# A decayed scan with layer norm and a quantized feed-forward layer: another first stage, with eight scan matmuls a batch instead of ten and a partial sum on GpSimd

## What is computed

```python
x = x + layernorm(x) * r
h = relu(quant_linear(layernorm(x), w1, b1))     # w1: 2048 x 512
x = x + quant_linear(h, w2, b2)                  # w2: 512 x 2048
# quant_linear: input rounded to 0..255 steps of s_in = max(input)/255 over the WHOLE input,
#   weight rounded to int8 with a scale per output channel, bias rounded to steps of s_in*s_w
```

## Time and profile before

| | |
|---|---|
| median of three runs | 1306.49 us |
| the profiled execution, its own time | 1307.37 us |
| its span, first to last instruction | 1305.6 us |
| mean granted TensorE clock, share of full speed | 0.979 |
| busy: PE, DVE, ACT, POOL | 1229.4, 909.8, 992.6, 291.0 us |
| moved by DMA | 460.23 MB, 353 GB/s in the mean |
| last operations on y in the first stage (DVE) end | 344.5 us |
| first hidden product starts | 358.7 us |
| second stage's last sums, third stage's first product | 832 us, 838.4 us |

### The profile page before, as it was taken

How to read it: one execution, slowest core, us unless ns; L and a number is a source line. 1 busy time by engine, 2 the same in 40 slices (tenths; PEclk the granted TensorE clock), 3 DMA queues, 4 the chain that set the end, 5 groups by cost and what they waited for, 6 DMA issues and landing times. The chain is left out here.

```text
span 1305.6 us, 17104 instructions
## 1 busy us (share of the span) xinstructions
PE 1229.4 (94%) x5386; PEld 564.2 (43%) x5386; DVE 909.8 (70%) x1314; ACT 992.6 (76%) x1403; POOL 291.0 (22%) x777
## 2 busy tenths in 40 slices
PE   6768999999599999999999999799999999999998
PEld 2333443434344444444444444344444444444443
DVE  5979999999667777777777777555545545444446
ACT  5688787877767777777777776688888777778794
POOL 2859999999600000000000000000000000000000
PEclk9888999999899999999999999899999999999999
DMA  9887999997489999999999997699999999999997
GB/s 356 330 320 262 343 335 349 328 350 287 184 298 358 368 350 347 363 362 361 349 354 363 363 356 297 246 341 414 415 415 415 415 415 416 415 416 416 416 352 260
DMA packets 136127, 460.23 MB, mean 353 GB/s; under 512 B 10852, under 2 KB 10872, under 8 KB 123512
## 3 DMA queue, kind: packets, MB, share of 16 engines
q1 hardware_dynamic: 82680, 276.86, 54.0%
q10 hardware_dynamic: 53376, 182.47, 39.3%
HBM read 266.35 MB, written 192.94 MB: 352 GB/s over the span
## 5 line engine op out<-in xcount | busy, mean ns | idle before, releaser
L881 PE MATMUL ps<-w2T,xq 128*128 128x512 f16 x2048 | 450.2, 381 | 11.9 <-ACT xq L593 11.4
L839 PE MATMUL ps<-xq,w1T 128*128 128x512 f16 x2048 | 449.8, 381 | 1.4 <-DVE xq L717 1.4
L593 ACT ACTIVATE xq<-xq,hb,hs 128x512 f16<-128x512 f32 x494 | 358.5, 802 | 83.2 <-PE ps L881 61.6
L708 DVE TENSOR_REDUCE work<-xq 128x2 f32<-128x1024 f32 x255 | 311.0, 1220 | 127.0 <-ACT xq L546 127.0
L546 ACT ACTIVATE xq<-ps 128x1024 f32<-128x1024 f32 x255 | 260.9, 1023 | 123.8 <-PE ps L839 123.5
L818 PE MATMUL ps<-xq,work 128*128 128x512 f32 x640 | 291.3, 613 | 30.0 <-ACT xq L481 19.6
L881 PEld LDWEIGHTS ps<-w2T,xq 128*128 128x128 f16 x2048 | 199.3, 98 | 262.8 <-ACT xq L593 26.0
L839 PEld LDWEIGHTS ps<-xq,w1T 128*128 128x128 f16 x2048 | 199.5, 98 | 237.7 <-issue 3.3
L818 PEld LDWEIGHTS ps<-xq,work 128*128 128x128 f32 x640 | 122.8, 195 | 196.1 <-issue 146.1
L756 DVE TENSOR_TENSOR work<-ps,cs_bc 128x512 f32<-128x512 f32 x128 | 87.1, 689 | 98.0 <-PE ps L881 90.8
L481 ACT ACTIVATE xq<-ps,rstd 128x512 f32<-128x512 f32 x128 | 77.9, 688 | 62.1 <-POOL rstd L448 56.3
(11 more groups left out here) (105 smaller groups left out, 577.4 us busy)
## 6 DMA issues: line engine op xcount, KB each, us to landing
hidden_scratch<-xq SPq DMA_DIRECT2D x240, 512.0 KB, 6.1
xq<-hidden_scratch ACTq DMA_DIRECT2D x220, 512.0 KB, 19.8
xq<-in_x_dram SPq DMA_DIRECT2D x32, 1024.0 KB, 7.8
x_scratch<-xq SPq DMA_DIRECT2D x32, 1024.0 KB, 5.7
xq<-in_ctx_dram ACTq DMA_DIRECT2D x31, 1024.0 KB, 5.6
work<-x_scratch ACTq DMA_DIRECT2D x29, 1024.0 KB, 7.9
work<-x_scratch SPq DMA_DIRECT2D x25, 1024.0 KB, 8.3
out_dram<-work SPq DMA_DIRECT2D x24, 1024.0 KB, 15.0
```

Of the source, the lines that this page charges most:

```text
L593: act.activation(hq[c % HQ], src[:, c % 2, :], ACT.Relu, bias=hb[:, q:q + 1], scale=hs[:, q:q + 1]).then_inc(h_scaled, 1)
L708: dve.tensor_reduce(hmax[:, b * NF + 2 * q:b * NF + 2 * q + 2], src, AX.X, ALU.max).then_inc(kept_maxed, 1)
L839: last = pe.matmul(bank, w1T[:, k, f * P:(f + 1) * P], xq_rows(b, k), start=(k == 0), stop=(k == KD - 1))
L881: last = pe.matmul(acc_bank(s, i), src[:, i * P:(i + 1) * P], w2T[:, q, :], start=first, stop=final)
```

## The change

The numbers of the first stage are made another way. ACT adds the negative mean to `x` in place and makes `1 + rstd * scan` from PSUM, and DVE makes `y = (x - mean) * (1 + rstd * scan)` in one multiplication with a row maximum. This y lacks the row's mean of `x`, which the second layer norm does not see; the means are kept in `nmean1` and subtracted when the bias is added to the output (`scalar_tensor_tensor` in place of `tensor_tensor`, 128 instructions). All `bn_stats` of `x` are DVE's, three batches ahead. GpSimd makes mean and deviation of two batches together, on 8 columns. It also makes `carried = 0.9^128 * kv0 + kv1` of each batch's squares, in two operations on 128x512, so that tiles 2 and 3 need two and three matmuls: 1+2+2+3 = 8. The scan rotates through six PSUM banks. Weights come in eight quarters of 1 MB, one every second batch from batch 2 on, and both weights are done inside the stage. `x` has eleven slots and `ctx` three; the last eleven batches of y stay in their slots, are quantized first and straight from there, and six of them are stored to DRAM in the second stage only. PE turns a quantized batch tile by tile as the tiles come.

```diff
-XS = 4
-ACT_TILES = 2
-AHEAD = 2
-
+XS = 11
+CS = 3
+RING = 4
+LATE = 6
+LEAD = 5
+BIAS_AT = 21
 HELD = 2
 NXQ = 3
 NKEEP = 12
 XC = 4
+NX = 3
...
+    parked = list(range(NB - XS, NB))
+    order_b = [b for n in range(XS - NX, XS) for b in parked if b % XS == n]
+    order_b += [b for b in parked if b not in order_b]
+    order_b += list(range(NB - XS))
+    late = list(range(NB - LATE, NB))
...
+    x_groups = [[0], [1]] + [[j, j + 1] for j in range(2, NB, 2)]
+    y_groups = [[j, j + 1] for j in range(0, NB - 2, 2)] + [[NB - 2], [NB - 1]]
+    x_group = {j: g for g, js in enumerate(x_groups) for j in js}
+    y_group = {j: g for g, js in enumerate(y_groups) for j in js}
+    quarters = [(w, k) for w in range(2) for k in range(4)]
+
+    def weights_at(j):
+        m = j // 2 - 1
+        return [m] if j % 2 == 0 and 0 <= m < len(quarters) else []
...
+            def load_x(j):
+                if j == XS - 1:
                     sp.wait_ge(dve_step, 1)
-                if not is_first(j, XS):
-                    sp.wait_ge(x2_stored[n], g * 16)
-                sp.dma_start(xt[n], x_rows[bass.ds(j, 1)].rearrange("b p i d -> (b p) i d")).then_inc(x_loaded[n], 16)
-                for w, h in weight_halves(j):
-                    rows = (NF, KD)[w]
-                    part = slice(h * rows // 2, (h + 1) * rows // 2)
-                    sp.dma_start(w_stage[w].rearrange("p (c d) -> p c d", c=rows)[:, part, :],
-                                 (w1_rows, w2_rows)[w][:, part, :]).then_inc(w_loaded[w][h], 16)
-                if isinstance(j, int) and j == 2:
+                if j >= XS:
+                    sp.wait_ge(stats2_in, j - XS + 1)
+                    x2_is_stored(sp, j - XS)
+                sp.dma_start(xt[j % XS], x_rows[j]).then_inc(x_loaded[j % XS], 16)
+
+            def load_weights(m):
+                w, k = quarters[m]
+                wait_count(sp, w_int, m - 1)
+                if w == 0:
+                    sp.dma_start(w_stage[m % 2].rearrange("p (c d) -> p c d", c=4), w1_rows[:, 4 * k:4 * k + 4, :]).then_inc(w_loaded[m % 2], 16)
+                else:
+                    sp.dma_start(w_stage[m % 2], w2_rows[:, k, :]).then_inc(w_loaded[m % 2], 16)
+
+            def store_x2(b):
+                sp.wait_ge(x2_done, (b + 1) * NI)
+                sp.dma_start(x2_dram[b], xt[b % XS].rearrange("p i d -> p (i d)")).then_inc(x2_stored[b % XS], 16)
...
+            for j in range(NB):
+                if j + LEAD < NB:
+                    load_x(j + LEAD)
+                for m in weights_at(j + 2):
+                    if m > 0:
+                        load_weights(m)
+                if j > 0 and j - 1 not in late:
...
+                if order_b[b] in late:
+                    store_x2(order_b[b])
...
-            def second_stats(j, n):
-
-                cols = bass.ds(j * NI, NI)
-                wait_count(gp, stats2_ready, j)
-                gp.wait_ge(stats2_in, j + 1)
-                mean = pw2[:, 8, :]
-                var = row_stats(pw2, st2[:, n], mean, ln2_step, j * 4)
-                gp.wait_ge(ln2_step, j * 4 + 4)
-                gp.tensor_tensor(pw2[:, 9, :], var, var, ALU.add)
-                gp.tensor_tensor(zrow[:, cols], rowmax[:, n, :], mean, ALU.subtract).then_inc(stats2_used, 1)
-                gp.tensor_tensor(mean2[:, cols], pw2[:, 0, :], half[:, :], ALU.mult)
...
+            def x_stats(g):
+                js = x_groups[g]
+                wait_count(gp, stats1_ready, g)
+                gp.wait_ge(stats1_in, js[-1] + 1)
+                var = row_stats(pw1, stats_of(st1, js), nmean1[:, columns(js)], neg_half)
+                gp.tensor_tensor(rstd1[:, columns(js)], var, neg_half[:, 0:len(js) * NI], ALU.pow).then_inc(stats1_ready, 1)
+
+            def y_stats(g):
+                js = y_groups[g]
+                wait_count(gp, stats2_ready, g)
+                gp.wait_ge(stats2_in, js[-1] + 1)
+                var = row_stats(pw2, stats_of(st2, js), mean2[:, columns(js)], half)
+                gp.tensor_tensor(zrow[:, columns(js)], stats_of(rowmax, js), mean2[:, columns(js)], ALU.subtract)
+                gp.tensor_tensor(rstd2[:, columns(js)], var, neg_half[:, 0:len(js) * NI], ALU.pow).then_inc(stats2_ready, 1)
+
+            def carry(j):
+                gp.wait_ge(ctx_squared, j + 1)
+                wait_count(gp, scan_ready, (j - 1) * NI)
+                into, kv = carried[j % 2], ct[j % CS]
+                step(gp.tensor_scalar(into[:, 0, :], kv[:, 0, :], DECAY ** P, None, ALU.mult))
+                gp.tensor_tensor(into[:, 0, :], into[:, 0, :], kv[:, 1, :], ALU.add).then_inc(carry_ready, 1)
...
+            carry(0)
+            x_stats(x_group[0])
+            x_stats(x_group[1])
+            for j in range(NB):
+                if j % 2 == 1 and j + 1 < NB:
+                    x_stats(x_group[j + 1])
+                if j + 1 < NB:
+                    carry(j + 1)
+                if j % 2 == 0 and j >= 2:
+                    y_stats(y_group[j - 1])
+                for m in weights_at(j):
+                    round_weights(m)
+            y_stats(y_group[NB - 2])
...
-            def tile_stats(j, n, g):
-
-                for m, i in enumerate(range(NI - ACT_TILES, NI)):
-                    at = j * (2 * ACT_TILES) + 2 * m
-                    if m == 0:
-                        act.wait_ge(x_loaded[n], (g + 1) * 16)
-                    wait_count(act, act_step, at)
-                    mean = st1[:, n, i, 1:2]
-                    act.activation(unused, xt[n][:, i, :], ACT.Copy, scale=1.0 / D, accum_out=mean).then_inc(act_step, 1)
-                    act.wait_ge(act_step, at + 1)
-                    act.activation(st1[:, n, i, 4:5], mean, ACT.Copy)
-                    last = act.activation(unused, xt[n][:, i, :], ACT.Square, bias=mean, scale=-1.0, accum_out=st1[:, n, i, 2:3])
-                    last.then_inc(act_step, 1)
-
-            def scale_scan(j, n):
-
-                act.wait_ge(stats1_ready, j + 1)
-                for i in range(NI):
-                    act.wait_ge(scan_ready, j * NI + i + 1)
-                    wait_count(act, x2_done, (j - 2) * NI + i + 1)
-                    act.activation(rs[n % 2][:, i, :], ps[:, i, :], ACT.Copy, scale=rstd1[:, n, i:i + 1]).then_inc(scan_scaled, 1)
...
+            def load_ctx(j):
+                wait_count(act, scan_ready, (j - CS + 1) * NI)
+                act.dma_start(ct[j % CS], ctx_rows[j]).then_inc(ctx_loaded[j % CS], 16)
+
+            def square(j):
+                act.wait_ge(ctx_loaded[j % CS], 16 * (j // CS + 1))
+                act.activation(ct[j % CS], ct[j % CS], ACT.Square).then_inc(ctx_squared, 1)
+
+            def factors(j, i):
+                u = j * NI + i
+                if i == 0:
+                    act.wait_ge(stats1_ready, x_group[j] + 1)
+                xi = xt[j % XS][:, i, :]
+                act.activation(xi, xi, ACT.Identity, bias=nmean1[:, u:u + 1])
+                act.wait_ge(scan_ready, u + 1)
+                wait_count(act, x2_done, u + 1 - 2 * NI)
+                act.activation(g1[j % 2][:, i, :], scan_bank(j, i), ACT.Identity, bias=ones[:, 0:1],
+                               scale=rstd1[:, u:u + 1]).then_inc(scan_scaled, 1)
...
+            load_ctx(1)
+            load_ctx(2)
+            square(0)
+            for j in range(NB):
+                factors(j, 0)
+                factors(j, 1)
+                if j + 1 < NB:
+                    square(j + 1)
+                factors(j, 2)
+                factors(j, 3)
+                if j + CS < NB:
+                    load_ctx(j + CS)
+                for m in weights_at(j - 1):
+                    int_weights(m)
+                for m in weights_at(j - 3):
+                    keep_weights(m)
+                if j == BIAS_AT + 1:
...
-                def product(i):
-                    dve.wait_ge(scan_scaled, j * NI + i + 1)
-                    dve.scalar_tensor_tensor(rs[n % 2][:, i, :], xt[n][:, i, :], mean1[:, n, i:i + 1], rs[n % 2][:, i, :],
-                                             ALU.subtract, ALU.mult).then_inc(prod_done, 1)
...
-                def add(i):
-                    dve.tensor_tensor_reduce(xt[n][:, i, :], rs[n % 2][:, i, :], xt[n][:, i, :], 1.0, -3.0e38, ALU.add, ALU.max,
-                                             rowmax[:, n, i:i + 1]).then_inc(x2_done, 1)
...
+            def product(j, i):
+                if i == 0 and j >= RING:
+                    dve.wait_ge(stats2_ready, y_group[j - RING] + 1)
+                dve.wait_ge(scan_scaled, j * NI + i + 1)
+                xi = xt[j % XS][:, i, :]
+                dve.tensor_tensor_reduce(xi, g1[j % 2][:, i, :], xi, 1.0, -3.0e38, ALU.mult, ALU.max,
+                                         rowmax[:, j % RING * NI + i:j % RING * NI + i + 1]).then_inc(x2_done, 1)
+
+            def y_stats(j, i):
+                dve.wait_ge(x2_done, j * NI + i + 1)
```

(36 more changed lines are left out.)

373 lines of the change are left out of this document (140 added, 233 removed).

## The result

The changed kernel takes 1308.7 us (median of 16 runs, 1305.3 to 1312.1) against 1305.9 us for the kernel before, timed beside it (16 runs, 1303.8 to 1307.1). The ratio is 1.0021, 95% interval 1.0013 to 1.0029. That is slower by 0.2%: in practice the same time, where 1262 us was forecast. The profiled execution took 1307.2 us.

A forecast was written before the change was run, and what follows sets the result against it. Only the first stage, POOL-paced before, would shorten, no engine then standing out: 21.5 + 16 x 9.5 + 13 x 8.2 + 3 x 7.4 = 302.3 us, 42.2 saved. With 1.5 + 1.5, 45 off 1307.4: 1262 us; range 1240 to 1295.

The forecast's parts named there:

- PE 7.1 us: First stage, steady batch: PE's 16 records at 0.443 us each take 7.1 us, against 8.86 for 20 before.
- the steady period of 8.2 us: First stage, batches without weights: engines between 7.1 and 8.0 us, none standing out, so 8.2 us a batch.
- Who interferes with whom: Skill's rule on DVE two-input operations contending with GpSimd: at worst 2.1 us added to DVE a batch, about 1302 us.
- the power on 8 columns: POOL's power of -0.5 in the paired statistics: between 1.0 and 1.8 us, taken as 1.8, twice for two batches.
- the addition: POOL's two-input operation on 128x512 in the carried sum: in no row, between 0.78 and 1.9 us, taken as 1.3.
- the scaling: POOL's multiplication in the carried sum: priced like the weight rounding L439, 0.78 us.
- Four nearly equal: 9.5: First stage, batches with weights: DVE 9.1, POOL 8.8, ACT 9.05, DMA 9.2 us, so 9.5 a batch.
- rival A: The forecast itself: no engine stands out, 8.2 and 9.5 us a batch, range 1249 to 1275 us; chance 0.62.
- Rival D: First stage: PE, resting a fifth of each batch, loses its clock; 1346 us with half the batches slow; chance 0.04.
- Rival B: First stage: POOL stays the pacer, the new sums taking what pairing gave; 1297 us; chance 0.17.
- Rival C: First stage: DMAs set the pace at 361 GB/s, with three `ctx` slots refilled late; 1280 us; chance 0.12.
- The ends: First stage's start 21.5 us against 18.95; going into the second stage, two savings of 1.5 us each.

The follow-up runs named there:

- e1: Changed kernel with GpSimd's rounding of each weight piece a batch later, after the sum, and ScalarE's and TensorE's weight steps a batch later too: 1263.5 us, ratio 0.9669.
- e9: Changed kernel with an addition of zero as second operation in GpSimd's scaling of the carried tile: 1291.7 us, ratio 0.9892.
- e10: Changed kernel with the weight chain (rounding and later steps) a batch later and GpSimd's scaling given an addition of zero: 1248.1 us, ratio 0.9551.

## Why the prediction was wrong

- **PE 7.1 us, the steady period of 8.2 us**: right in the main. PE's 16 records take 6.9 us where nothing interrupts them (0.43 each). The period is right where no long gap interferes, 8.0 to 8.2 from 302 to 334 us; one batch, 22, took 12.7. POOL is no longer the pacer: its short operations take 0.20 us, now and then 0.65 to 0.73.
- **DVE**: 0.60 from one operation to the next holds. The product takes 0.69 us alone, 0.78 in the mean of 128, 0.4 us a batch for contention where 0.5 was taken. The rule "Who interferes with whom" (the Trainium skill, "SBUF — State Buffer") at its worst gave 1302 us, near the measured time, but that is luck, for the cause is not there: e1 keeps both POOL operations as they are beside the same products and takes 1263.5 us.
- **POOL**: the power on 8 columns took 1.64 to 1.67 us as a rule (1.8 taken), the addition 1.27 (1.3), the scaling 1.50 (0.78 taken). That last term was mis-sized by 0.72 us a batch. Its price is 17 us in the changed kernel (e9) and 15 in the one with the order mended (e1 to e10).
- **"Four nearly equal: 9.5"** is the step that failed, 11.9 measured. It compared what each engine has to do and never asked in which order POOL does it. POOL's `round_weights(m)` of batch j waits for DVE's last act in batch j, and `x_stats` and `carry` of the next batch are behind it. The program shows this; the prediction names no wait of POOL for the scale. With the rounding a batch later the period is 9.3 (e1), and the kernel takes 1263.5 us where 1262 was forecast. That this is so near is partly luck: e1 has the scaling at 1.50 us, and with one near the price that was taken (e10, 0.62) the period is 8.9 and the time 1248.1, at the lower bound of rival A. So the sum of work was some 14 us too long, the scaling costs 15 and the order, for which the forecast had nothing, 45: 1262 - 14 + 15 + 45 = 1308.
- **Rival D**: right in its result (not faster) and half in its means. It was set aside since "the gaps I expect are 1 to 2 us"; those with weights were 5.9 to 8.2. PE did lose its clock, for some 6 us in each pair of batches, which is worth 17 us. The argument that "a slow PE has no gaps" failed, since it is the sum that makes the gap, not PE's own speed.
- **Rival B** had POOL as pacer by load, which e1 refutes. **Rival C**: ACT waited 5.3 us for `ctx` in the whole kernel, once, so no; its other half, the DMAs as the limit, may be met in e10, but at 396 GB/s and not at 361. The Trainium skill's 358 GB/s ("DMA: Bandwidth & Descriptors", "Where 436 GB/s comes from") is exceeded there for 100 us.
- **The ends**: start 22.3 (21.5 forecast); from y's last statistics to the first hidden product 11.4 us in place of 14.2, 2.8 of the 3.0 forecast. The second stage takes 479.2 us (479.7 before), the third some 2.7 us less in this profile.
- **The chances**: 0.02 for the same time and 0.05 for a slower kernel were too low. That no engine stood out was read as a stage that none holds up for long; it can as well be a stage in which a ring of waits forms.
